# A tokenizer, a recurrence and a mixture of experts: the recurrence put between the two score halves

## The reference

```python
reduce_feats = x.mean((3, 5)).reshape(b, c, hw).transpose(0, 2, 1)      # mean of a patch
q  = _ln(reduce_feats, ln_q_w, ln_q_b) @ Wq.T                           # 8 heads of 32
kv = _ln(unf, ln_kv_w, ln_kv_b) @ Wkv.T                                 # of all 16 pixels
attn = softmax(q * scale . k, axis=-1)                                  # over the 16 pixels
h = reduce_feats + (attn . v) @ proj_w.T + proj_b
h = concatenate([cls_tok, h], axis=1)                                   # 32 x 257 x 256
# recurrence over the images, each token a sequence of 32 steps
h_new = tanh(layernorm(h_t) @ W_ih.T + h_old @ W_hh.T + b_ih + b_hh);  h = h + h_new
# mixture of 8 experts, the best 2 for each token
rw, re = top_k(softmax(t @ router_w.T), 2);  out = t + sum_e combine[:, e] * (gelu(t @ w1[e] + b1[e]) @ w2[e] + b2[e])
```

## Time and profile before

| what | value |
| --- | --- |
| median of 3 runs | 1443.47 us (1440.27 to 1452.13) |
| the profiled execution | 1442.62 us, its span 1440.8 us |
| TensorE busy | 1311.7 us (91%) |
| VectorE, ScalarE, GpSimd busy | 1030.9, 816.1, 712.2 us |
| DMA | 423.7 MB, mean 294 GB/s |

### The profile page before, as it was taken

One profiled execution on the slowest core, in us unless ns is written; L12 is line 12 of the kernel. 1 busy time (PEld: TensorE's weight loads), 2 busy tenths in 40 slices (PEclk: granted clock), 3 DMA queues, 4 the chain that ended last, 5 costly groups with the idle time before them and its releaser, 6 DMA issues. The chain is left out here.

```text
span 1440.8 us, 61906 instructions
## 1 busy us (share of the span) xinstructions
PE 1311.7 (91%) x25169; PEld 1071.9 (74%) x25169; DVE 1030.9 (72%) x2724; ACT 816.1 (57%) x1999; POOL 712.2 (49%) x852
## 2 busy tenths in 40 slices
PE   4799999999999999999999999999997999999960
PEld 3577787878777777877787877777775899987750
DVE  4677777777777677787777767668865676688874
ACT  1456555655665555655565655555556677766630
POOL 2234343434444344343366666664331477776675
PEclk9999999999999999999999999999998999999985
DMA  8999889999999889998899999999643689999986
GB/s 275 405 316 323 298 296 304 309 301 301 300 303 310 281 291 293 304 301 281 285 341 343 349 346 334 334 332 322 212 142 110 203 286 292 293 316 326 307 282 217
DMA packets 186614, 423.70 MB, mean 294 GB/s; under 512 B 23968, under 2 KB 89312, under 8 KB 186208
## 3 DMA queue, kind: packets, MB, share of 16 engines
q1 hardware_dynamic: 170336, 380.27, 77.8%
q0 software_dynamic: 14048, 38.16, 8.5%
q10 hardware_dynamic: 1952, 1.32, 0.4%
HBM read 332.26 MB, written 87.39 MB: 291 GB/s over the span
## 5 line engine op out<-in xcount | busy, mean ns | idle before, releaser
L1132 DVE BATCH_NORM_STATS2 st<-xp 128x6 f32<-128x512 f32 x512 | 340.1, 696 | 16.6 <-DMA xp<-xpix 16.1
L672 POOL TENSOR_TENSOR rs_px<-px_ve,half_neg 128x16 f32<-128x16 f32 x64 | 187.0, 2922 | 177.7 <-DVE px_ve L1137 177.7
L786 ACT ACTIVATE zT<-bank 128x512 f32<-128x512 f32 x256 | 138.6, 597 | 91.8 <-PE bank L975 91.8
L779 ACT ACTIVATE z_s<-bank 128x512 f32<-128x512 f32 x256 | 138.7, 597 | 79.0 <-PE bank L965 79.0
L934 PE MATMUL bank<-xc,u 128*32 128x64 f32 x8192 | 149.4, 220 | 28.6 <-issue 27.9
L934 PEld LDWEIGHTS bank<-xc,u 128*32 128x32 f32 x8192 | 131.5, 110 | 55.4 <-issue 44.7
L760 ACT ACTIVATE u<-bank 128x512 f32<-128x512 f32 x256 | 132.1, 603 | 49.7 <-PE bank L913 49.7
L1421 POOL DMA_INDIRECT y<-ys_dram,slot x130 | 129.1, 993 | 58.2 <-issue 38.4
L657 POOL TENSOR_TENSOR q_rs<-q_ve,half_neg 128x1 f32<-128x1 f32 x64 | 35.1, 548 | 242.2 <-DVE q_ve L1149 242.2
L975 PE MATMUL bank<-ident,z_s 128*128 128x128 f32 x1024 | 150.1, 280 | 2.9 <-ACT z_s L779 1.6
L413 POOL DMA_INDIRECT xs_dram<-xrow,slot x130 | 129.6, 997 | 38.0 <-issue 34.8
(11 more groups left out here) (178 smaller groups left out, 3076.6 us busy)
## 6 DMA issues: line engine op xcount, KB each, us to landing
xp<-xpix SPq DMA_DIRECT2D x256, 512.0 KB
xc<-xg SPq DMA_DIRECT2D x256, 512.0 KB
xc<-xs_dram SPq DMA_DIRECT2D x86, 256.0 KB
ys_dram<-y_s SPq DMA_DIRECT2D x86, 256.0 KB
xs_dram<-zero SPq DMA_DIRECT2D x57, 384.0 KB, 5.6
base_dram<-h SPq DMA_DIRECT2D x65, 128.0 KB, 5.7
rows_dram<-tok SPq DMA_DIRECT2D x65, 128.0 KB
hb<-base_dram SPq DMA_DIRECT2D x65, 128.0 KB, 4.1
```

The costliest lines, as they stand in the source:

```text
L672: pool.tensor_tensor(rs_px[:, :], px_ve[:, :], half_neg[:, :], ALU.pow).then_inc(s["px_done"], 1)
L779: act.activation(z_s[:, r, 2 * half:2 * half + 2, :].rearrange("p a c -> p (a c)"), BIG[2 * r + half][:, :], ACT.Copy).then_inc(s["z_done" ...
L786: act.activation(zT[:, c, :, :].rearrange("p h (a r t) -> p r h a t", r=2, t=TS)[:, r, :, :, :], BIG[f][:, :].rearrange("p (a h t) -> p h ...
L1132: dve.bn_stats(st[:, j, :], xp[u.x][:, 2 * j:2 * j + 2, :].rearrange("p i c -> p c i")).then_inc(s["st_done"], 1)
```

## The change

No instruction is added and no tile or bank is changed. The order of the calls in `slot` is changed on SyncE, ScalarE, TensorE and VectorE; in the slots that have every part, this is what differs:

```diff
 # SyncE
                     wait(sp, s["rT_ps"], u, 1, 1)
+                    if end:
+                        wait(sp, s["nt_ps"], z, 1, 1)
                     load_xp(sp, w.x, w.k + XBUF, [1])
-                    wait(sp, s["zt_ps"], w, 4, 2)
+                    if end:
+                        wait(sp, s["h_ps"], z, 1, 1)
                     load_xp(sp, w.x, w.k + XBUF, [2])
-                    wait(sp, s["rn_ps"], u, 1, 1)
+                    wait(sp, s["s_ps"], v, 1, 1)
                     load_xp(sp, w.x, w.k + XBUF, [3])
+                if more_xc:
+                    wait(sp, s["s_ps"], v, 1, 1)
+                    if back:
+                        wait(sp, s["zt_ps"], w, 4, 2)
+                    load_xc(sp, v.c, v.k + XC, [0])
...
                 if more_xc:
-                    wait(sp, s["s_ps"], v, 1, 1)
+                    if back:
+                        wait(sp, s["zt_ps"], w, 4, 4)
+                    load_xc(sp, v.c, v.k + XC, [1])
                     wait(sp, s["q_ps"], u, 1, 1)
-                    load_xc(sp, v.c, v.k + XC, [0])
+                    load_xc(sp, v.c, v.k + XC, [2])
...
                 if more_xc:
-                    if back:
-                        wait(sp, s["a_ps"], w, 1, 1)
-                    load_xc(sp, v.c, v.k + XC, [1])
                     wait(sp, s["u_ps"], u, 1, 1)
-                    load_xc(sp, v.c, v.k + XC, [2])
-                    if back:
-                        wait(sp, s["pj_ps"], w, 1, 1)
                     load_xc(sp, v.c, v.k + XC, [3])
 # ScalarE
                     mean_out(act, u)
+                if end:
+                    xn_out(act, z)
+                    hidden(act, z)
                 if back:
                     zT_out(act, w, 0)
...
+                if mid:
+                    exps(act, v)
                 if front:
                     q_out(act, u)
-                if mid:
-                    exps(act, v)
-                if end:
-                    xn_out(act, z)
                 if back:
                     a_out(act, w)
...
                     route_turned(act, u.k - 4, FB)
-                if end:
-                    hidden(act, z)
-                if late:
+                if late and not mid:
                     route_logits(act, u.k - 4, FB)
...
                     z_out(act, v, [0, 1])
+                if late and mid:
+                    route_logits(act, u.k - 4, FB)
 # TensorE
                     means(pe, u)
+                if end:
+                    turn_xn(pe, z)
                 if mid:
                     score(pe, v, 0)
+                if end:
+                    recur(pe, z, 0)
+                    recur(pe, z, 1)
+                if mid:
+                    score(pe, v, 1)
                 if back:
                     turn_z(pe, w, 0)
                     turn_z(pe, w, 1)
+                if front:
+                    turn_rn(pe, u)
                 if mid:
-                    score(pe, v, 1)
+                    fold_patches(pe, v)
                 if back:
                     turn_z(pe, w, 2)
-                if front:
-                    turn_rn(pe, u)
-                if back:
                     turn_z(pe, w, 3)
-                if mid:
-                    fold_patches(pe, v)
-                if end:
-                    turn_xn(pe, z)
                 if front:
                     queries(pe, u)
...
                     turn_p(pe, v)
-                if end:
-                    recur(pe, z, 0)
-                    recur(pe, z, 1)
                 if back:
                     project_out(pe, w)
+                if end:
+                    turn_h(pe, z)
+                if mid:
+                    weigh(pe, v, front, 0)
                 if late:
                     logits(pe, u.k - 4, FB)
-                if end:
-                    turn_h(pe, z)
...
                 if mid:
-                    weigh(pe, v, front, 0)
                     weigh(pe, v, front, 1)
 # VectorE
+                if end:
+                    token_norm(dve, z)
                 if front:
                     stats(dve, u, [0, 1, 2])
...
                     unmask(dve, v)
-                if end:
-                    token_norm(dve, z)
```

More of the change, by code:

```diff
@@ L591, in slot @@
             def slot(sp, u, front, mid, back, end, late):
-                v, w, t = u.before(), u.before(2), u.k - 4
+                v, w, z, t = u.before(), u.before(2), u.before(3), u.k - 4
                 more_xp, more_xc = back and w.k + XBUF < UNITS, mid and v.k + XC < UNITS
```

## The result

| | before | changed |
| --- | --- | --- |
| median | 1444.24 us (1440.27 to 1452.13, 4 runs) | 1509.82 us (1506.34 to 1514.5, 4 runs) |
| ratio, 95% interval | | 1.0469 [1.043, 1.0508] |
| span of the profiled execution | 1440.8 us | 1507.1 us |

The change makes the kernel 65.6 us slower. I had forecast 1451 us, no difference that can be measured, in a range up to 1470: the forecast is wrong, and no rival reaches the result either.

A forecast was written before the change was run, and what follows sets the result against it. TensorE's own list was taken to set the pace. A slot: 15.68+0.73+0.04+0.20 = 16.65 us against 16.52, +0.13 times 61 = +8 us, so about 1451 us; 8 in 10 range 1438 to 1470.

The forecast's parts named there:

- Step 1: Before `fold_patches`: TensorE's wait for the mask goes, -0.20 us in an undisturbed slot, 0 in a disturbed one.
- Step 2: Before `weigh`: a new wait for the four `u_out` copies of the projection, +0.73 us a slot in 61 slots.
- Step 3: Mostly in the scores: waits for instruction blocks not yet arrived shrink from 0.64 to 0.20 us a slot.
- Edits at nearly nothing: `route_logits`, `xn_out`, `token_norm` and load data: almost no new waiting, 0.04 us a slot for `route_logits`, the rest 0.
- Rival B: ScalarE becomes late along its chain, at `values` and `route_logits`: +15 us more, 1466 us; chance 0.15.
- Rival A: Idle stretches stay at 0.64 us a slot, through DMA load or another cause: +35 us, 1478 us; chance 0.13.

The follow-up runs named there:

- the lightened kernel: Kernel before, loading one of 128 partitions of `xp` and `xc` once buffers are filled: 1413.07 us; with first score half and z turns alternating too: 1415.48 us.
- the loads in the middle: The faster order with all loads issued between the first turn of z and the end of the recurrence: 1459.67 us, ratio 1.0069.
- the faster order: Kernel before with `fold_patches` directly ahead of `values`, `turn_p` behind the recurrence, the norm heading VectorE's slot, `xn_out` ahead of `q_out`: 1435.64 us, ratio 0.9925.

## Why the prediction was wrong

**The step that failed is the first sentence of its second part:** "TensorE's instructions stay the same, so its own work in a slot does." Only its first half holds. The same 25,169 matmuls take TensorE longer, since four more switches a slot stand between them. In the undisturbed slot they cost 17.11-15.88 = 1.23, less 0.79 for `u`, plus 0.20 for the mask: **0.64 us**, 0.16 each, times 61 = 39 us. The two runs that moved one pair of switches each give 0.66. I had the tile shapes before me in every row, and used the duration of a group as if it were its own, whatever stands beside it.

The Trainium skill states the rule, on its page "TensorEngine Tiling (Array Packing)", under "Key Properties": changing the tiling mode, as opposed to the tile, drains TensorE. The rows agree, with a cost at each such change and weight loads that sit idle 0.41 us at some of them: 0.14 us for each of the two in the lightened kernel, 0.10 to 0.19 over all the runs. I looked for rules on waits and on the fetch, and not for one on what a matmul's neighbour does to it.

- **Step 1, the mask (-0.20): right.** The waits of the changed kernel have no row in which `L948` waits for `sm`. The run with the recurrence put back shows the condition: it is the recurrence's delay of the second half that pays for it.
- **Step 2, the copies (+0.73): right.** 0.72 in the timeline, 0.79 when taken away.
- **Step 3, the blocks' waits (0.20 left): half right.** I gave the scores 12 us and they and the other "issue" rows of matmuls have 11.6 (9.3+1.8+0.5). But the mean slot is 0.42 above the undisturbed one (17.52-17.11), 25 us in 59 slots. The other 10 us of before, which I had called thinly spread, I left out of the sum; they are still there (25-11.6 = 13). This is 0.22 us a slot, 13 us in all. They are thinly spread only in part. Held against the undisturbed slot group by group, the changed kernel's trace has 13.0 us more in the score halves (9.3 of it shown as idle) and 6 us more in other groups over 57 slots, and 5.6 us in a single one, 22.66 us long, where the routing's ranks are computed as well. Under light loads the other slots' excess is gone and that one takes 19.95 us, 2.8 over the rest: this part is work and no wait for the fetch. The kernel before has such a slot too, of 18.81 us with or without the loads, so a part of its 38 us, which the prediction called idle time, was work.
- **Edits at nearly nothing: right.** `means` does not wait for `lg_all`, and `turn_xn`, `recur` and `values` wait for nobody, or once, by 0.2 us. Rival B (ScalarE late along its chain) did not happen.
- **The sum.** Forecast slot 16.65; plus 0.64 for the switches, 0.22 for the thin stretches, 0.06 for the copies, less 0.04 for `route_logits`, makes 17.53, measured 17.52. The 0.64 and the 0.22 are read from the same trace, so that this closes is no further proof; the 0.66 of the two runs is. The forecast's 1451 plus 61 x 0.87 = 53 gives 1504; the remaining 6 us lie outside the slots 3 to 62, nearly all behind them (1507.1-1095.51 = 411.6 us against 1440.8-1036.04 = 404.8), where I haven't followed them.
- **Rival A (the stretches stay)** had the fetch late "by the load on the DMA queues, whatever TensorE does meanwhile". Its cause is right, as the lightened kernels show; that TensorE's pace plays no part is not, since the changed order has less of this idle time than the old one with the same loads (11.2 against 27.9 us) and the faster one more (35.8). And the rule of the Trainium skill that I had set against step 3, on its page "Runtime: NRT & Kernel Launch", under "Instruction fetch mechanics", that the fetch is hidden, does not hold here, and the measurement decides: the fetch is hidden at a DMA share of 0.18 (1.2 us idle) and not at 0.92 (27.9 us).

What stays open: why a switch costs 0.10 us at one place and 0.19 at another (the kinds of tile shape and the groups around them differ, and no run varies one alone), and how long the packet of a block waits behind the loads before it starts (my expectation for the loads in the middle had the wrong sign).

## What to carry to other kernels

Before moving groups on TensorE, write the tile shape beside each and count how often it changes along the list, before and after; a change costs about 0.15 us here and no wait of the matmuls shows it (look at the weight loads' "issue" rows), so an order with fewer changes is worth looking for by itself. When something is moved from between a producer and its reader, work out the reader's new wait from the slot in which the thing is absent: that term was right to 0.06 us here. And where a stretch of idle time depends on how fast the engine runs, expect it to take back part of each gain and of each loss (14 of 25 us of the faster order's gain here, and 18.6 us of the change's loss), and put all of it into the sum, the thin part too.

## What the runs showed of the hardware

- A change of the tile's shape costs TensorE 0.10 to 0.19 us, 0.14 in the cleanest pair. The matmuls show it as busy time; at some places, as `turn_xn` and the logits of the changed kernel, the weight load behind the change is idle for 0.41 us.
- TensorE's instruction fetch stalls the score matmuls when the DMA queues are busy: 27.9 us of it at a DMA share of 0.92, 1.2 us at 0.18; nothing between was measured. The loads that the lightened kernel leaves out cost the kernel before 1441.19-1413.07 = 28 us (ratio 0.9786 [0.9721, 0.9851], both on one chip).
- Loads in a burst are worse for it than the same loads spread out: 55.2 us idle in the scores against 29.0, and 1459.67 against 1434.01 us. That is so in the faster order; in the changed one the two placements that were tried gave the same time.
